# A local-attention stage whose operations are re-ordered across tiles on every engine, with the input split cut per tile and three slots for V

## The chip, the core and the metric

The kernel runs on one core of a Trainium2 chip. The core has TensorE (PE in the profile; its weight loads are PEld), VectorE (DVE), ScalarE (ACT), GpSimd (POOL), and SyncE (SP), which here only issues DMAs. Each engine works through its own list of instructions in order; semaphores tie the lists together. The metric is the device time of one execution in microseconds, the median of several. Before the change it is 907.86 us (three runs, 907.16 to 908.72). A difference under 0.2% (1.8 us) is no measurable change.

## The reference

`x` is 4 sequences of 1024 tokens with 128 features. The result is `x + s * silu(f)`, where both branches take the layer norm of `x`.

```
s: q, k, v = xn @ Wqkv.T, 16 heads of 8, rope on q and k,
   causal attention inside blocks of 32 tokens, @ Wout.T
f: two layers (DEPTH = 2), each
   h   = shift_token(x)                    # upper 64 features from the token before
   q, k, v = split(h @ wqkv)               # 8 heads of 64, INNER = 512
   q, k = l2norm(q) * qs, l2norm(k) * ksc, then rotary with xpos scaling
   sim  = 8 * q k^T, window of 64 tokens: own block and the block before, causal
   x   += softmax(sim) v @ wo              # "local attention"
   h   = layernorm(shift_token(x)) * lg + lb
   a, g = split(h @ w1 + b1)
   x   += (a * gelu(g)) @ w2 + b2
```

## The kernel before

Tokens lie along the free dimension of `X` (128 features x 4096 tokens). The program runs a small-head attention first (32 tiles of 128 tokens), and then twice a **local stage** (32 tiles of 128 tokens) and a feed-forward stage (8 chunks of 512 tokens). The change is in the local stage.

**One tile m of the local stage** goes through these operations. PE projects q, k and v (three fp32r products each, into PSUM banks 0, 1 and 2, from `split`, the input as a high and a low part). ACT squares q and k, DVE sums the squares per head, ACT makes the inverse norms of them (three tiny operations). DVE multiplies q by its cosine and sine tables and adds (`qr`), POOL scales it. DVE scales k (`kn`), POOL rotates it (`kA`, `kB`, `kr`). PE transposes `qr` and `kr` into bank 3, and ACT copies them to `qT` and `kT`. PE computes the scores into banks 4 and 5, DVE takes the maxima (`nmax`), ACT the exponentials with their sums (`prob`), DVE the reciprocals, POOL the normalised probabilities. PE transposes those in two halves (bank 6), ACT copies (`pT`), PE multiplies by the values (bank 7, called PV below), ACT copies (`oT`), PE multiplies by `wo` (bank 3 again), DVE adds the result to `X`.

**The block before.** A query block also looks at the 64 tokens before it. So each tile needs the second half of the last tile's keys in front of its own (`kT[..., 0:WIN]`), and values shifted by half a tile (`VB`). SP makes these by DMA from SBUF to SBUF. In step n of SP's list (`back`) it

1. issues the key copy of tile n, which the scores of tile n+1 wait for (semaphore `k_prev`);
2. once V of tile n is there, issues the first VB copy;
3. waits until PV of tile n-1 is done (`l_o`), since that product reads the slot of VB which is written next, and issues the second VB copy;
4. issues the two shifted copies of a finished tile of `X` into `XS[1]`, the feed-forward stage's input.

Ahead of item 1 step n waits until the `XS[1]` copies issued in step n-1 have landed. SP has one list, so all this is strictly in a row.

**Order of the work.** The lists are written out by hand: on each engine a function `local(n, par)` says what the engine does in turn n, and the turns follow each other. In the kernel before, turn n of PE is: q projection of tile n+2, q transposes of n, first probability transposes of n-1, k projection of n+2, k transposes of n, v projection of n+1, second probability transposes of n-1, scores of n, output product of n-2, PV of n-1. So PV of tile n-1 stands in the same turn as the scores of tile n. Slots alternate with the parity of the tile (V, VB, kT, qT, qr, kr, prob).

Of the kernel before, what the change touches and what calls it, by code (L numbers as in the profile page):

```python
# [78 lines left out]
def build(nc, a, out):  # L79
    with ExitStack() as ctx:  # L80
# [52 lines left out]
        V = sb("V", [P, 2, INNER])  # L133
# [101 lines left out]
        l_qk = sem("l_qk")  # L235
        l_v = sem("l_v")
        l_sq = sem("l_sq")
        l_qm = sem("l_qm")
        l_norm = sem("l_norm")
# [8 lines left out]
        l_tr = sem("l_tr")  # L248
        l_tre = sem("l_tre")
# [3 lines left out]
        l_score = sem("l_score")  # L253
        l_max = sem("l_max")
        l_exp = sem("l_exp")
        l_rinv = sem("l_rinv")
        l_prob = sem("l_prob")
        l_pT = sem("l_pT")
        l_pTe = sem("l_pTe")
# [48 lines left out]
        def _(sp):  # L308
# [49 lines left out]
            for L in range(DEPTH):  # L358
# [4 lines left out]

                def back(n, par):
                    nxt = 1 - par
                    base = L * TILES
                    turned, done = held(2 * (base + n + 1)), held(base + n + 1)
                    scored, pv1 = held(2 * (base + n)), held(base + n)
                    copied = held(xs_before_local(L) + 32 * (n - 2))
                    if live(n, -3, TILES):  # L370

                        sp.wait_ge(xs_dma, copied)
                    if live(n, 0, TILES):
                        sp.wait_ge(l_tre, turned)
                        wait(sp, l_score, scored)
                        sp.dma_start(kT[:, nxt, :, 0:WIN], kT[:, par, :, P:P + WIN]).then_inc(k_prev[nxt], 16)
                        sp.wait_ge(l_ve, done)
                        sp.dma_start(VB[64:P, par, :], V[0:64, par, :]).then_inc(v_prev[par], 16)
                        wait(sp, l_o, pv1)
                        sp.dma_start(VB[0:64, nxt, :], V[64:P, par, :]).then_inc(v_prev[nxt], 16)  # L380
                    if live(n, -2, TILES):
                        copy_shifted(XS[1], n - 2, P, x_before_local(L) + n - 1)

                if L == 0:

                    sp.wait_ge(zeros_made, 2)
                    sp.wait_ge(windows_zero, 1)
                    sp.dma_start(kT[:, 0, :, 0:WIN], kT[:, 1, :, P:P + WIN]).then_inc(k_prev[0], 16)
                    sp.dma_start(VB[0:64, 0, :], V[64:P, 1, :]).then_inc(v_prev[0], 16)
                steps(0, TILES + 1, back)  # L390
# [22 lines left out]
        def _(pe):  # L413
# [104 lines left out]
            def layer(L, tail):  # L518
# [6 lines left out]
                def project(c, hi, lo, made):  # L525

                    mm3(ps[:, c, :], hi, lo, wqkv[:, 0, c * INNER:(c + 1) * INNER],
                        wqkv[:, 1, c * INNER:(c + 1) * INNER]).then_inc(made, 1)

                def transposed(n, par, src, ready):  # L530
                    pe.wait_ge(ready, base + n + 1)
                    for c in range(4):
                        last = turn(ps[:, 3, c * P:(c + 1) * P], src[:, par, c * P:(c + 1) * P])
                    last.then_inc(l_tr, 1)

                def local(n, par):
                    nxt = 1 - par
                    now, ahead = [[split[:, (m // TPC) % 2, i, (m % TPC) * P:(m % TPC + 1) * P] for i in range(2)]
                                  for m in (n + 2, n + 1)]
                    if live(n, 2, TILES):  # L540
                        pe.wait_ge(l_split, L * CHUNKS + (n + 2) // TPC + 1)
                        wait(pe, l_qm, base + n + 2)
                        project(0, *now, l_qk)
                    if live(n, 0, TILES):

                        wait(pe, x_new, (x_before_local(L) + n - 2) if not isinstance(n, int) or n > 2 else 0)
                        transposed(n, par, qr, l_qn)

                    def scores():
                        if live(n, 0, TILES):  # L550
                            pe.wait_ge(l_tre, 2 * (base + n + 1))

                            pe.wait_ge(k_prev[par], 16 * ((base + n) // 2 + 1))
                            wait(pe, l_exp, 8 * (base + n))

                            first = 1 if par else live_mask(n)
                            half = [slice(64 * i, 64 * i + 64) for i in range(2)]
                            for w, grp in ((0, 0), (1, 1), (1, 0), (0, 1)):
                                kind = 1 if w else first
                                mm(ps[half[w], 4 + grp, :], ident_bf[half[grp], half[grp]],  # L560
                                   lmask[half[grp], bass.ds(kind * CHUNK, CHUNK)], True, False)
                            for s in range(4):
                                for w, grp in ((0, 0), (1, 1), (1, 0), (0, 1)):
                                    last = mm(ps[half[w], 4 + grp, s * P:(s + 1) * P],
                                              qT[half[grp], par, s, half[w]],
                                              kT[half[grp], par, s, 64 * w:64 * w + P], False, True)
                                    if s == 3 and w != grp:
                                        last.then_inc(l_score, 1)

                    def turned_probs(grp):  # L570
                        if live(n, -1, TILES):

                            pe.wait_ge(l_prob, 2 * (base + n - 1) + grp + 1)
                            wait(pe, l_pTe, 2 * (base + n - 1) + grp)
                            for s in range(4):
                                last = turn(ps[:, 6, s * P:(s + 1) * P], prob[:, nxt, grp, s * P:(s + 1) * P])
                            last.then_inc(l_pT, 1)

                    def output():

                        if not live(n, 0, TILES):
                            pe.wait_ge(x_new, x_before_local(L) + n - 2)
                        pe.wait_ge(l_oe, base + n - 1)
                        if live(n, 0, TILES):
                            pe.wait_ge(l_tre, 2 * (base + n + 1))
                        for c in range(4):
                            last = mm(ps[:, 3, 0:P], wo[:, c, :], oT[:, par, c * P:(c + 1) * P], c == 0, c == 3)
                        last.then_inc(l_y, 1)

                    scores_done = isinstance(n, int) and n == TILES  # L590
                    turned_probs(0)
                    if scores_done:
                        bias_products()
                        output()
                    if live(n, 2, TILES):
                        wait(pe, l_kn, base + n + 2)
# [862 lines left out]
```

## Time and profile before

| | |
|---|---|
| median of three runs | 907.86 us |
| profiled execution | 909.96 us, its span 908.2 us |
| PE busy | 800.1 us (88% of the span) |
| DVE busy | 664.4 us (73%) |
| ACT busy | 654.3 us (72%) |
| POOL busy | 523.9 us (58%) |
| mean granted TensorE clock | 0.972 |
| local stages | first maxima to last maxima: 190 to 446 us, and 551 to 808 us |

A row of a group or of the timeline names the line, the engine, the operation, output and inputs, and after an "x" how many instructions it merges. In the timeline the two numbers ahead are the start and the duration in us; the brackets at the end say how long the engine stood idle before and what released it. SPq is SP's queue, and its duration is that of the issue, not that of the transfer. `PEclk` is the granted clock: 1.00 is 2.4 GHz and 0.50 is 1.2 GHz.

### The profile page before, as it was taken

The page shows a single profiled execution, that of the slowest core. Times are in us where ns is not written, and L with a number is a line of the kernel's source. Part 1 is how long each engine was busy: PE and PEld are TensorE (multiplying, and loading weights), DVE is VectorE, ACT ScalarE, POOL GpSimd, SP SyncE. Part 2 cuts the span into 40 slices and gives each one's busy share as a digit, 9 for nine tenths or more (in the row PEclk, how much of TensorE's full clock was granted, in tenths as well). Part 3 has the DMA queues.
Part 4 walks back from the last instruction along what each step waited for, and adds up shares of the span by engine and source line. Part 5 has one row for each costly group of instructions (what it writes and reads, how often), then busy time and mean ns, then how long its engine had stood idle before and what let it go on. Part 6 is the DMA issues. An engine that isn't in the chain of part 4 may idle for free.

```text
span 908.2 us, 26049 instructions
## 1 busy us (share of the span) xinstructions
PE 800.1 (88%) x9848; PEld 610.5 (67%) x9848; DVE 664.4 (73%) x1347; ACT 654.3 (72%) x2053; POOL 523.9 (58%) x521
## 2 busy tenths in 40 slices
PE   4779999779999999999989887999999999988985
PEld 1458778557777778777756545777877777775652
DVE  1577998677887787877457767778787788745765
ACT  2337777479899899889743337989988998974463
POOL 0363333078888888888511017888888888951100
PEclk8899999889999999999999998999999999999997
DMA  9110001012222222222201121222222222222001
GB/s 308 44 45 3 4 4 41 3 47 55 57 57 63 55 58 55 60 57 63 51 18 24 29 63 37 64 53 58 57 61 56 62 52 58 58 51 100 1 36 58
DMA packets 64704, 48.24 MB, mean 53 GB/s; under 512 B 40410, under 2 KB 50948, under 8 KB 64068
## 3 DMA queue, kind: packets, MB, share of 16 engines
q1 hardware_dynamic: 64580, 46.57, 19.9%
q8 instruction: 80, 1.31, 0.6%
q14 instruction: 44, 0.36, 0.1%
HBM read 10.63 MB, written 2.10 MB: 14 GB/s over the span
## 4 chain that ended last, share of the span: by engine, by line
PE 56%; ACT 17%; DVE 16%; issue 7%; POOL 1%; DMA 1%; SPq 1%; DVEq 0%; ACTq 0%; POOLq 0%
PE ps L415 47%; PE ps L425 9%; ACT prob L880 6%; DVE nmax L1130 3%; ACT sq L822 3%; DVE nt L1158 2%; ACT V L849 2%; ACT oT L831 2%; DVE split L970 2%; ACT kT L856 1%; ACT pT L826 1%; DVE prob L1217 1%; DVE split L968 1%; DMA awo<-in_awo 1%; ACT qT L841 1%
## 5 line engine op out<-in xcount | busy, mean ns | idle before, releaser
L880 ACT ACTIVATE prob<-ps,nmax 128x128 f32<-128x128 f32 x512 | 181.8, 374 | 36.7 <-DVE nmax L1130 36.7
L415 PE MATMUL ps<-wqkv,split 128*128 128x512 f32 x576 | 188.2, 438 | 14.2 <-DVE split L970 10.1
L1348 POOL TENSOR_TENSOR prob<-prob,rinv 128x512 f32<-128x512 f32 x128 | 133.9, 1046 | 88.4 <-DVE rinv L1116 45.8
L415 PEld LDWEIGHTS ps<-wqkv,split 128*128 128x128 f32 x576 | 97.5, 195 | 33.5 <-DVE split L970 10.2
L1130 DVE TENSOR_REDUCE nmax<-ps 128x4 f32<-128x512 f32 x128 | 83.6, 686 | 48.3 <-PE ps L415 48.3
L425 PE MATMUL ps<-ident,prob 128*128 128x128 f32 x640 | 98.3, 276 | 13.9 <-POOL prob L1348 13.1
L880 ACT ACTIVATION_READ_ACCUMULATOR prob<-ps,nmax 128x1 f32 x512 | 109.0, 213 | 0.0
L1359 POOL TENSOR_TENSOR qr<-qr,ss 128x512 f32<-128x512 f32 x64 | 66.9, 1046 | 53.7 <-DVE qr L1142 53.7
L425 PEld LDWEIGHTS ps<-ident,prob 128*128 128x128 f32 x640 | 76.2, 142 | 28.3 <-POOL prob L1348 17.4
L415 PE MATMUL ps<-oT,wo 128*128 128x128 f32 x512 | 73.9, 287 | 22.0 <-ACT oT L831 22.0
L826 ACT ACTIVATE pT<-ps 128x512 f32<-128x512 f32 x128 | 80.0, 625 | 10.7 <-PE ps L425 9.1
L415 PE MATMUL ps<-split,w 128*128 128x512 f32 (+1 forms) x288 | 81.4, 427 | 6.6 <-DVE prob L1217 6.3
L415 PEld LDWEIGHTS ps<-oT,wo 128*128 128x128 f32 x512 | 62.1, 191 | 37.3 <-ACT oT L831 36.3
L822 ACT ACTIVATE sq<-ps 128x512 f32<-128x512 f32 x128 | 81.8, 640 | 5.1 <-PE ps L415 5.0
L1370 POOL TENSOR_TENSOR kr<-kA,kB 128x512 f32<-128x512 f32 x64 | 82.4, 1287 | 5.0
L1364 POOL TENSOR_TENSOR kA<-kn,lrot 128x512 f32<-128x512 f32 x64 | 81.8, 1278 | 0.0
L1313 POOL TENSOR_TENSOR qr<-ident,rstd 128x512 f32<-128x512 f32 x16 | 16.6, 1042 | 99.1 <-DVE rstd L962 96.0
L415 PEld LDWEIGHTS ps<-split,w 128*128 128x128 f32 (+1 forms) x288 | 50.4, 180 | 31.1 <-DVE prob L1217 10.1
L1330 POOL TENSOR_TENSOR prob<-D,hmask 128x512 f32<-128x512 f32 x32 | 35.1, 1097 | 59.5 <-PE ps L415 59.4
L1142 DVE TENSOR_TENSOR qr<-tA,tB 128x512 f32<-128x512 f32 x64 | 68.6, 1072 | 0.0
L415 PE MATMUL ps<-pT,VB 128*64 128x64 f32 x1024 | 66.3, 228 | 1.5 <-issue 1.5
L415 PE MATMUL ps<-kT,qT 64*64 64x128 f32 x2048 | 66.8, 269 | 0.0
(139 smaller groups left out, 1871.9 us busy)
## 6 DMA issues: line engine op xcount, KB each, us to landing
VB<-V SPq DMA_DIRECT2D x129, 128.0 KB, 2.4
kT<-kT SPq DMA_DIRECT2D x65, 128.0 KB, 2.4
XS<-X SPq DMA_DIRECT2D x32, 128.0 KB, 2.3
XS<-X SPq DMA_DIRECT2D x128, 32.0 KB, 1.9
D<-in_xT SPq DMA_DIRECT2D x8, 256.0 KB, 4.4
XS<-in_xT SPq DMA_DIRECT2D x2, 1024.0 KB, 6.7
out_T<-XS SPq DMA_DIRECT2D x8, 256.0 KB, 2.0
raw<-in_wqkv SPq DMA_DIRECT2D x2, 768.0 KB, 4.4
```

What stands on the lines that cost most here:

```text
L415: return nc.tensor.matmul(o, l, r, start=start, stop=stop, skip_group_check=True)
L425: return nc.tensor.matmul(o, i, ident[:], is_transpose=True, start=True, stop=True, skip_group_check=True)
L822: nc.scalar.activation(sq[:, c, :], ps[:, c, :], ACT.Square).then_inc(l_sq, 1)
L826: nc.scalar.activation(pT[:, grp, :], ps[:, 6, :], ACT.Copy).then_inc(l_pTe, 1)
L880: nc.scalar.activation(prob[:, par, grp, s * P:(s + 1) * P], ps[:, 4 + grp, s * P:(s + 1) * P], ACT.Exp, bias=nmax[:, par, grp * 4 + s:grp ...
L1130: v.tensor_reduce(nmax[:, par, 4 * grp:4 * grp + 4], ps[:, 4 + grp, :].rearrange("p (s k) -> p s k", s=4), AX_X, ALU.max, negate=True).the ...
L1142: v.tensor_tensor(qr[:, nxt, :], tA[:], tB[:], ALU.add).then_inc(l_qr, 1)
L1330: g.tensor_tensor(kexp[:, par, :].rearrange("p (b h k) -> p b h k", b=BLKS, h=INGRP), part(kR, n, P).rearrange("p (b k) -> p b k", b=BLKS) ...
L1348: g.tensor_tensor(p4, p4, rinv[:, slot, 4 * grp:4 * grp + 4].unsqueeze(2).broadcast_to([P, 4, P]), ALU.mult).then_inc(l_prob, 1)
L1359: g.tensor_tensor(hd(qr[:, nxt, :]), hd(qr[:, nxt, :]), ss[:, nxt, 0:8].unsqueeze(2).broadcast_to([P, HEADS, HD]), ALU.mult).then_inc(l_qn, 1)
L1364: g.tensor_tensor(hd(kA[:]), hd(kn[:]), row8(2, pos, 0, HD), ALU.mult)
L1370: g.tensor_tensor(kr[:, nxt, :], kA[:], kB[:], ALU.add).then_inc(l_kr, 1)
```

## The change

Every operation stays on its engine and is as large as before, but for one: the split of the input into high and low part, which was made for 512 tokens at a time (two operations on DVE for four tiles), is made for each tile (eight operations on DVE for four tiles), eight turns ahead. The combined semaphores are replaced by one per operation, and `V` has three slots where it had two; `VB` still has two. Each engine's turn n has a new order, and the operations in it belong to tiles that lie further apart:

| operation | tile in PE's turn n, before | after |
|---|---|---|
| q / k / v projection | n+2 / n+2 / n+1 | n+4 / n+3 / n+1 |
| q and k transposes | n | n+1 |
| scores | n | n |
| probability transposes | n-1 | n-2 |
| PV | n-1 | n-2 |
| output product | n-2 | n-4 |

There are 40 turns (-4 to 35) where there were 36 (-2 to 33). On SP the shifted copies are those of tile n-5 (before n-2). The rest of SP's list is in the same order. The core of the diff:

```
-        V = sb("V", [P, 2, INNER])
+        V = sb("V", [P, 3, INNER])
         VB = sb("VB", [P, 2, INNER])
...
                 def back(n, par):
-                    if live(n, -3, TILES):
-                        sp.wait_ge(xs_dma, copied)
+                    nxt, done = 1 - par, base + n + 1
+                    if live(n, -6, TILES):
+                        sp.wait_ge(xs_dma, xs_before_local(L) + 32 * (n - 5))
                     if live(n, 0, TILES):
-                        sp.wait_ge(l_tre, turned)
-                        wait(sp, l_score, scored)
+                        sp.wait_ge(l_tk, done)
+                        wait(sp, l_score[1], done - 1)
                         sp.dma_start(kT[:, nxt, :, 0:WIN], kT[:, par, :, P:P + WIN]).then_inc(k_prev[nxt], 16)
                         sp.wait_ge(l_ve, done)
-                        sp.dma_start(VB[64:P, par, :], V[0:64, par, :]).then_inc(v_prev[par], 16)
-                        wait(sp, l_o, pv1)
-                        sp.dma_start(VB[0:64, nxt, :], V[64:P, par, :]).then_inc(v_prev[nxt], 16)
-                    if live(n, -2, TILES):
-                        copy_shifted(XS[1], n - 2, P, x_before_local(L) + n - 1)
+                        sp.dma_start(VB[64:P, par, :], V[0:64, done % 3, :]).then_inc(v_prev[par], 16)
+                        wait(sp, l_o, done - 1)
+                        sp.dma_start(VB[0:64, nxt, :], V[64:P, done % 3, :]).then_inc(v_prev[nxt], 16)
+                    if live(n, -5, TILES):
+                        copy_shifted(XS[1], n - 5, P, x_before_local(L) + n - 4)
...
+                def scores(m):                       # PE
...
+                        pe.wait_ge(l_tq, base + m + 1)
+                        pe.wait_ge(l_tk, base + m + 1)
+                        pe.wait_ge(k_prev[m % 2], 16 * ((base + m) // 2 + 1))
...
+                def local(n, par):                   # PE
+                    q_turned(n + 1)
+                    k_projected(n + 3)
+                    probs_turned(n - 2, 0)
+                    q_projected(n + 4)
+                    k_turned(n + 1)
+                    scores(n)
+                    probs_turned(n - 2, 1)
+                    output(n - 4)
+                    v_projected(n + 1)
+                    values_summed(n - 2)
...
+                def local(n, par):                   # ACT
+                    v_copied(n)
+                    k_copied(n + 1)
+                    norm_floor(n + 3)
+                    q_squared(n + 4)
+                    norm_log(n + 3)
+                    probs_copied(n - 2, 1)
+                    norm_inverse(n + 3)
+                    exponentials(n, 0)
+                    exponentials(n, 1)
+                    q_copied(n + 2)
+                    o_copied(n - 2)
+                    k_squared(n + 4)
+                    probs_copied(n - 1, 0)
...
+                def input_high(m):                   # DVE
...
+                        v.tensor_copy(split[:, (m // TPC) % 2, 0, bass.ds((m % TPC) * P, P)],
+                                      shifted(XS[0], m, P)).then_inc(split_hi, 1)
...
+                def local(n, par):                   # DVE
+                    q_cos(n + 3)
+                    input_high(n + 8)
+                    q_sin(n + 3)
+                    inverse_sums(n - 1, 0)
+                    q_rotated(n + 3)
+                    q_summed(n + 3)
+                    k_summed(n + 3)
+                    inverse_sums(n - 1, 1)
+                    maxima(n, 0)
+                    maxima(n, 1)
+                    k_scaled(n + 3)
+                    input_low(n + 8)
+                    added_to_x(n - 4)
...
+                def local(n, par):                   # POOL
+                    q_scaled(n + 3)
+                    k_sin(n + 3)
+                    normalised(n - 1, 1)
+                    k_cos(n + 3)
+                    k_rotated(n + 3)
+                    normalised(n, 0)
```

The instructions in a row on two engines. First PE in the middle of the first local stage, before: from the scores to PV, the products `ps<-pT,VB` and `ps<-pT,V`. `ident,prob` are probability transposes, `ident,qr` and `ident,kr` those of q and k, `wqkv,split` the projections, `lmask` and `kT,qT` the scores, `oT,wo` the output product.

```order
L425 MATMUL ps<-ident,prob 128x128 [waits l_pTe,l_prob]
L425 MATMUL ps<-ident,prob 128x128 x3
L415 MATMUL ps<-lmask,ident_bf 64x512 [waits l_exp,k_prev1,l_tre]
L415 MATMUL ps<-lmask,ident_bf 64x512 x3
L415 MATMUL ps<-kT,qT 64x128 x16
L415 MATMUL ps<-oT,wo 128x128 [waits l_tre,l_oe]
L415 MATMUL ps<-oT,wo 128x128 x3
L415 MATMUL ps<-pT,VB 64x64 [waits l_ve,v_prev0,l_pTe,l_oe]
```

The same engine and place after the change:

```order
L417 MATMUL ps<-lmask,ident_bf 64x512 [waits l_exp0,k_prev1,l_exp1,l_tk,l_tq]
L417 MATMUL ps<-lmask,ident_bf 64x512 x3
L417 MATMUL ps<-kT,qT 64x128 x16
L427 MATMUL ps<-ident,prob 128x128 [waits l_pTe0,l_prob1]
L427 MATMUL ps<-ident,prob 128x128 x3
L417 MATMUL ps<-oT,wo 128x128 [waits l_tk,l_oe]
L417 MATMUL ps<-oT,wo 128x128 x3
L417 MATMUL ps<-wqkv,split 128x512 [waits l_ve,l_split]
L417 MATMUL ps<-wqkv,split 128x512 x2
L417 MATMUL ps<-pT,VB 64x64 [waits l_ve,l_pTe1,v_prev1,l_pTe0,l_oe]
```

The second probability transposes and the v projection, which stood ahead of the scores, now stand between them and PV. PV before is that of the tile one ahead of the scored one, and after that of two ahead. What PE does after PV, until the next scores, is now this:

```order
L417 MATMUL ps<-pT,V 64x64 x2
L427 MATMUL ps<-ident,qr 128x128 [waits x_new,l_qn]
L427 MATMUL ps<-ident,qr 128x128 x3
L417 MATMUL ps<-wqkv,split 128x512 [waits l_kn,l_split]
L417 MATMUL ps<-wqkv,split 128x512 x2
L427 MATMUL ps<-ident,prob 128x128 [waits l_pTe1,l_prob0]
L427 MATMUL ps<-ident,prob 128x128 x3
L417 MATMUL ps<-wqkv,split 128x512 [waits l_sqq,l_qm,l_split]
L417 MATMUL ps<-wqkv,split 128x512 x2
L427 MATMUL ps<-ident,kr 128x128 [waits l_tq,l_kr]
L427 MATMUL ps<-ident,kr 128x128 x3
L417 MATMUL ps<-lmask,ident_bf 64x512 [waits l_exp0,k_prev0,l_exp1,l_tk,l_tq]
```

Two projections and three groups of transposes are left there; before, the v projection and a fourth group stood there too.

Second, SP's list in the middle of the stage, before. `kT<-kT` is the key copy, the first `VB<-V` the copy within a tile, the second the one into the slot of the next tile, `XS1<-X` the shifted copies.

```order
L376 DMA kT<-kT 128x4x64 [waits l_score,l_tre,xs_dma]
L378 DMA VB<-V 64x512 [waits l_ve]
L380 DMA VB<-V 64x512 [waits l_o]
L348 DMA XS1<-X 64x128 [waits x_new]
L349 DMA XS1<-X 64x128
```

After the change:

```order
L378 DMA kT<-kT 128x4x64 [waits l_score1,l_tk,xs_dma]
L380 DMA VB<-V 64x512 [waits l_ve]
L382 DMA VB<-V 64x512 [waits l_o]
L353 DMA XS1<-X 64x128 [waits x_new]
L354 DMA XS1<-X 64x128
```

Nothing moved on SP, and the waits are the same kinds; but the PV and the scores between which these copies stand have moved apart on PE.

## Rows read from the trace of the kernel before

**Rows 1.** Busy us of the engines over 24 tiles of the first local stage.

```profile
223.61:422.11 198.50, 183.05 (x2424) 149.85 (x2424) 159.82 (x300) 181.17 (x649) 167.53 (x169) 1.00 0.24 58
```

**Rows 2.** Timeline of PE over one turn.

```profile
307.34 1.16 PE L415 MATMUL ps<-oT,wo 128*128 128x128 f32 x8 [0.39 <-ACT oT L831]
308.43 0.34 PE L415 MATMUL ps<-pT,VB 128*64 128x64 f32 x4
...
309.29 0.29 PE L415 MATMUL ps<-pT,V 128*64 128x64 f32 x4
309.51 0.97 PE L415 MATMUL ps<-wqkv,split 128*128 128x512 f32 x3
...
311.11 0.94 PE L415 MATMUL ps<-wqkv,split 128*128 128x512 f32 x3
311.88 0.60 PE L425 MATMUL ps<-ident,kr 128*128 128x128 f32 x4
312.26 0.96 PE L415 MATMUL ps<-wqkv,split 128*128 128x512 f32 x3
313.06 0.60 PE L425 MATMUL ps<-ident,prob 128*128 128x128 f32 x4
313.59 0.41 PE L415 MATMUL ps<-lmask,ident_bf 64*64 64x512 bf16 x4
...
315.27 1.16 PE L415 MATMUL ps<-oT,wo 128*128 128x128 f32 x8 [0.39 <-ACT oT L831]
```

**Rows 3.** Timeline of SP's queue after a PV, and at tile 30.

```profile
309.62 0.46 SPq L380 DMA_DIRECT2D VB<-V  x1
310.12 0.60 SPq L348 DMA_DIRECT2D XS<-X  x1
310.76 0.60 SPq L349 DMA_DIRECT2D XS<-X  x1
...
433.80 0.60 SPq L349 DMA_DIRECT2D XS<-X  x1
435.79 0.63 SPq L376 DMA_DIRECT2D kT<-kT  x1
```

**Rows 4.** The page's DMA issues: count, KB, median us from issue to landing.

```profile
kT<-kT SPq DMA_DIRECT2D x65, 128.0 KB, 2.4
```

**Rows 5.** Timeline of DVE: maxima of tiles 0 and 31, both layers.

```profile
190.12 1.29 DVE L1130 TENSOR_REDUCE nmax<-ps 128x4 f32<-128x512 f32 x2 [0.19 <-PE ps L415]
...
446.43 1.29 DVE L1130 TENSOR_REDUCE nmax<-ps 128x4 f32<-128x512 f32 x2 [4.08 <-PE ps L415]
...
550.75 1.29 DVE L1130 TENSOR_REDUCE nmax<-ps 128x4 f32<-128x512 f32 x2 [0.84 <-PE ps L415]
...
807.90 1.29 DVE L1130 TENSOR_REDUCE nmax<-ps 128x4 f32<-128x512 f32 x2 [4.08 <-PE ps L415]
```

**Rows 6.** Windows of 6 us from the start of a PE gap: busy, PEclk, DMA.

```profile
64.90:70.90 6.00, 2.52 (x43) 0.78 0.00 0
...
552.00:558.00 6.00, 3.64 (x39) 1.00 0.02 5
...
893.70:899.70 6.00, 3.19 (x6) 0.84 0.12 44
36.50:42.50 6.00, 4.54 (x16) 1.00 0.19 44
```

**Rows 7.** Timeline of PE behind the gap that ends at 193.74.

```profile
193.74 0.66 PE L425 MATMUL ps<-ident,prob 128*128 128x128 f32 x4 [2.35 <-POOL prob L1348]
194.15 1.26 PE L415 MATMUL ps<-wqkv,split 128*128 128x512 f32 x3
195.21 1.05 PE L425 MATMUL ps<-ident,kr 128*128 128x128 f32 x4
195.92 1.63 PE L415 MATMUL ps<-wqkv,split 128*128 128x512 f32 x3
197.34 0.92 PE L425 MATMUL ps<-ident,prob 128*128 128x128 f32 x4
```

More of the change, by code:

```diff
@@ L536, in local @@
[L536 to L557, printed above, removed]
-                            for w, grp in ((0, 0), (1, 1), (1, 0), (0, 1)):
[L559 to L585, printed above, removed]
@@ new lines, in scores @@
+                def scores(m):
+                    if 0 <= m < TILES:
+                        if m == 0:
+                            if L == 0:
+                                pe.wait_ge(a_done, TILES)
+                            else:
+                                pe.wait_ge(ffn_hid, NPART * L * CHUNKS)
+                        pe.wait_ge(l_tq, base + m + 1)
+                        pe.wait_ge(l_tk, base + m + 1)
+                        pe.wait_ge(k_prev[m % 2], 16 * ((base + m) // 2 + 1))
+                        wait(pe, l_exp[0], 4 * (base + m))
+                        wait(pe, l_exp[1], 4 * (base + m))
+                        first, par = min(m % TPB, 1), m % 2
+                        half = [slice(64 * i, 64 * i + 64) for i in range(2)]
+                        for w, grp in ((0, 0), (1, 1), (1, 0), (0, 1)):
+                            kind = 1 if w else first
+                            mm(ps[half[w], 4 + grp, :], ident_bf[half[grp], half[grp]],
+                               lmask[half[grp], bass.ds(kind * CHUNK, CHUNK)], True, False)
+                        for s in range(4):
+                            for w, grp in ((0, 0), (1, 1), (1, 0), (0, 1)):
+                                last = mm(ps[half[w], 4 + grp, s * P:(s + 1) * P],
+                                          qT[half[grp], par, s, half[w]],
+                                          kT[half[grp], par, s, 64 * w:64 * w + P], False, True)
+                                if s == 3 and w != grp:
+                                    last.then_inc(l_score[grp], 1)
@@ new lines, in probs_turned, with output @@
+                def probs_turned(m, grp):
+                    if 0 <= m < TILES:
+                        pe.wait_ge(l_prob[grp], base + m + 1)
+                        wait(pe, l_pTe[1 - grp], base + m + grp)
+                        for s in range(4):
+                            last = turn(ps[:, 6, s * P:(s + 1) * P], prob[:, m % 2, grp, s * P:(s + 1) * P])
+                        last.then_inc(l_pT[grp], 1)
+                def output(m):
+                    if 0 <= m < TILES:
+                        if m == 0:
+                            pe.wait_ge(wo_in, 16 * (L + 1))
+                        pe.wait_ge(l_oe, base + m + 1)
+                        if 0 <= m + 5 < TILES:
+                            pe.wait_ge(l_tk, base + m + 5 + 1)
+                        elif 0 <= m + 5 < TILES:
+                            pe.wait_ge(l_tq, base + m + 5 + 1)
+                        elif 0 <= m - 1 < TILES:
+                            pe.wait_ge(x_new, x_before_local(L) + m - 1 + 1)
@@ L586, in output @@
                         for c in range(4):
[L587 removed]
+                            last = mm(ps[:, 3, 0:P], wo[:, c, :], oT[:, m % 2, c * P:(c + 1) * P], c == 0, c == 3)
                         last.then_inc(l_y, 1)
[L590 to L594, printed above, removed]
@@ L864, in local, with o_copied, norm_floor @@
+                def o_copied(m):
+                    if 0 <= m < TILES:
+                        act.wait_ge(l_o, base + m + 1)
+                        wait(act, l_y, base + m - 1)
+                        nc.scalar.activation(oT[:, m % 2, :], ps[:, 7, :], ACT.Copy).then_inc(l_oe, 1)
+                def norm_floor(m):
+                    if 0 <= m < TILES:
+                        act.wait_ge(l_nq, base + m + 1)
+                        act.wait_ge(l_nk, base + m + 1)
                         nc.scalar.activation(lognt[:, 0, :], nt[:], ACT.Relu, bias=floor[:, 0:1]).then_inc(l_floor, 1)
-                    if live(n, -2, TILES) and not scores_done:
-                        output()
```

466 lines of the change are left out of this document (248 added, 218 removed).

## The prediction

> **What bounds the kernel now.** I read the share of busy time first, then the local stage by windows, then PE's timeline over one turn, then SP's queue, because what the change moves apart on PE is tied together by copies on that queue.
>
> The local stages make up 513 of the 908 us: from the first maxima to the last 256.3 us in the first layer and 257.2 us in the second [rows 5], for 31 intervals each. In the regular middle 24 tiles take 198.5 us, 8.27 us a tile. In them PE is busy 183.1 us, ACT 181.2, POOL 167.5 and DVE 159.8 [rows 1], so per tile 7.63, 7.55, 6.98 and 6.66 us. PE is the bound, nearly: one turn is 315.27 - 307.34 = 7.93 us, with one idle stretch of 0.39 us ahead of the output product, until ACT has copied `oT` [rows 2]. Without it a turn would be 7.54 us.
>
> SP's queue is not late before. After a PV it issues the second VB copy and the two shifted copies and then waits anyway, for the next tile's `kT` [rows 3]; the scores that wait for that key copy come almost a turn after it.
>
> **What the change does to that queue.** The loop to look at runs: PV of tile n-1, then on SP the second VB copy, the two shifted copies of tile n-5, the wait until these have landed, the key copy of tile n+1, then on PE the scores of tile n+2. Before, PV of tile n-1 was in turn n and those scores in turn n+2; what closed the loop was PV of tile n+1 in the same turn, so one pass advanced by two tiles and had two turns of time. After, PV of tile n-1 is in turn n+1, and behind the scores of tile n+2 comes PV of tile n, in the same turn n+2. One pass now advances by one tile only. A third V slot does nothing for it: VB has two slots still, and the queue is as strict as it was.
>
> The length of one pass, step by step:
> - PV ends at 309.29 + 0.29 = 309.58 [rows 2], the VB copy is issued at 309.62 [rows 3]: 0.04.
> - VB copy to first shifted copy 0.50, to the second 0.64 [rows 3].
> - Second shifted copy, issued at 433.80, to the key copy at 435.79 [rows 3]: 1.99. This is the one place of the regular kind where `kT` was ready first, so that the landing is what the queue waited for.
> - Key copy, issue to landing: 2.4 [rows 4].
> - PE: scores 315.27 - 313.59 - 0.39 = 1.29; four probability transposes 313.59 - 313.06 = 0.53; output product 308.43 - 307.34 = 1.09; v projection 313.06 - 312.26 = 0.80; PV until its end 309.58 - 308.43 = 1.15 [rows 2]. Together 4.86.
>
> SP's part is 5.57, the pass 10.43 us. That is above the 8.27 us of now and above what any engine needs. What PE has to do between PV and the next scores (two projections, three groups of transposes) took 312.26 - 309.51 = 2.75 us before [rows 2], so it ends long before the key copy lands, and PE then stands idle for about 5.57 - 2.75 + 0.07 = 2.9 us in every turn.
>
> The first shifted copy is issued in SP's step 5 and waited for first in step 6. Up to the scores of tile 6 a pass has neither the 0.64 nor the 1.99: 10.43 - 2.63 = 7.8 us. So of 31 intervals 6 cost 7.8 (46.8 us in all) and 25 the full pass.
>
> **The clock.** I then looked at what such a gap of PE does to its granted clock. The trace has nine gaps of PE of 2 us or longer (after the start of the kernel), at 64.9, 168.6, 176.4, 191.4, 516.4, 544.2, 552.0, 559.7 and 893.7. Over the six microseconds from their start the mean clock was 0.78 for the first and 0.84 for the last, and it stayed 1.00 only at 552.0; behind the five gaps of about 1.5 us, the first at 36.5, it was 1.00 [rows 6]. In eight of nine cases, then, the clock went down to its 1.2 GHz level and came back later. Behind the gap that ends at 193.74 the slow stretch reaches from about 194.2 to the transposes at 197.34, which still show 0.92 instead of 0.60 [rows 2, 7]: some 3.5 us of work. There k projection to k transposes took 195.21 - 194.15 = 1.06 where it takes 0.77, and those transposes 0.71 where they take 0.38 [rows 2, 7]. Work runs at about half speed, so 3.5 us of it lose 1.75. In the changed kernel the fall comes with the end of the gap, which is the start of the scores, and the slow stretch lies on the part of PE's turn that is in the loop. I take off 0.25 for falls that begin inside the gap and count eight in nine: 1.5 x 8/9 = 1.33 us a tile. The pass becomes 11.76 us.
>
> [...]
>
> **The other edits.**
> - Removed wait: the 0.39 us ahead of the output product goes, since its `oT` is now of four tiles back. Next late is the key copy, so this is worth nothing.
> - Order on ACT, DVE and POOL: with 7.55, 6.66 and 6.98 us of work in a turn of 11.8 each has over 4 us of room, and what the scores, transposes and PV take from them is made a turn ahead or in PE's gap. No cost. In a turn of 7.54 ACT would have no room at all; that matters only in the last rival.
> - Split per tile: eight instructions for four tiles instead of two. DVE's price per tile is unknown, between nothing and 1 us; either way hidden by DVE's 5 us of free time. Cost 0; without the cover up to 1 us x 64.
> - Third V slot and single semaphores: they take a wait from ACT that is not late. 0.
> - SP: the same five issues per step. The waits for V and `kT` are met before SP comes to them.
> - Filling and draining: four more turns per layer. At the start PE transposes the keys of tile 1 before it scores tile 0, so POOL's work on one more tile (6.98 us) lies ahead; I take 6. At the end there are two more passes through bank 3 (an output product, 1.16 us, and an addition each), and PV of the last tile waits for one more pass of SP's queue; I take 4. Together 10 a layer, between 0 (the attention's and the feed-forward's last work cover it) and 17; a gain is excluded, since turns are only added.
>
> **The sum.** A layer: 46.8 + 25 x 11.76 = 340.8 us from first to last maxima. Against 256.3 and 257.2 that is +84.5 and +83.6, together +168. With 20 for the ends it is +188 on the profiled execution's 909.96: 1098 us. The median of the runs is 2.1 us below the profiled execution, so 1096 us. Its own range: at a loss of 1.0 to 2.0 us a tile from the clock, and 0 to 34 for the ends, about 1060 to 1135.
>
> **Rivals.**
> - *The clock holds.* The gap of 2.9 us is there, but the matmuls around it keep the clock up, as at 552.0. The pass is 10.43: 46.8 + 260.8 = 307.6 a layer, +51.3 and +50.4, with the ends +122: 1030 us. For it: one case in nine, and a clock of 1.00 through the whole of rows 1. Against: the other eight.
> - *The landing of the shifted copies is not in the pass.* If SP could go on to the key copy at once, the pass would be 8.44 and the gap about 0.9 us, too short for the clock: 46.8 + 211.0 = 257.8, +2 over both layers, with the ends 930 us. For it: only one place shows the 1.99, and there the pieces of SP may have met by chance. Against: the wait is written ahead of the key copy, and it needs the copies just issued.
> - *The queue never decides, and PE runs without a gap (faster).* The place is the same: the key copy. If it is there when PE comes to the scores, a turn is 7.54 us: 31 x 7.54 = 233.7, -22.6 and -23.4, with the ends 26 us faster: 882 us. It decides from a pass under 7.54 on, which needs SP's part to be 2.7 us, half of what I read. For it: PE has 7.54 us of work, and all the other loops that I followed (bank 3, the norms, the probabilities) have time in such a turn. Against: the four rows of SP's part, each measured.
>
> **Chances.** The forecast 0.62, the clock holds 0.20, landing not in the pass 0.10, faster 0.08. A measurement of this kernel tells 0.2% (1.8 us) from no change. Faster then comes to 0.07, within it 0.01, slower 0.92. The range reaches down to the clock's rival and up to the top of the forecast's own: 1015 to 1135.
>
> **What would show it.** In the changed profile: turns of 7.8 us up to tile 6, then 11 to 12.5 us; PE busy far below 88% of a longer span; one idle stretch of 2.5 to 3 us per turn ahead of `lmask`, released by a DMA; a mean clock near 0.85 and 0.5 in many half-microseconds behind those gaps; SP's key copy 2 us behind the second shifted copy in every step, where before that happened rarely. The wait for `oT` is gone. It would be wrong if PE waited ahead of the scores for an engine, or if the key copy were issued early in the turn, and mis-sized if turns were near 10.4 with the clock at 1.00.

## The result and the profile after

The changed kernel takes 1070.11 us (median of four runs, 1065.85 to 1079.05) against 907.51 us: 1.180 times as long, 95% interval 1.1725 to 1.188. 1096 us were predicted, in a range of 1015 to 1135. The profiled execution has a span of 1066.9 us where it had 908.2.

The page: its busy times, and the granted clock in 40 slices.

```profile
span 1066.9 us, 26797 instructions
PE 830.5 (78%) x9848; PEld 633.6 (59%) x9848; DVE 677.9 (64%) x1443; ACT 646.6 (61%) x2053; POOL 549.4 (51%) x521
...
PEclk7999998799899989997799989999999999889997
```

The work is what it was: PE is busy 30 us more, most of it work at a low clock (a turn at a low clock below has 10.2 us of PE busy, a regular one 7.45); the other engines' busy times are near the old ones. The span has grown by 159 us, so nearly all of it is waiting. This is PE's timeline over one turn, in the stage's regular part; it answers to [rows 2].

```profile
331.16 0.60 PE L427 MATMUL ps<-ident,kr 128*128 128x128 f32 x4
334.49 0.41 PE L417 MATMUL ps<-lmask,ident_bf 64*64 64x512 bf16 x4 [2.73 <-issue]
...
335.70 0.66 PE L427 MATMUL ps<-ident,prob 128*128 128x128 f32 x4
336.19 1.06 PE L417 MATMUL ps<-oT,wo 128*128 128x128 f32 x8
337.01 0.95 PE L417 MATMUL ps<-wqkv,split 128*128 128x512 f32 x3
337.88 0.34 PE L417 MATMUL ps<-pT,VB 128*64 128x64 f32 x4
...
338.75 0.29 PE L417 MATMUL ps<-pT,V 128*64 128x64 f32 x4
338.96 0.66 PE L427 MATMUL ps<-ident,qr 128*128 128x128 f32 x4
...
344.65 0.41 PE L417 MATMUL ps<-lmask,ident_bf 64*64 64x512 bf16 x4 [2.72 <-issue]
```

The turn is 344.65 - 334.49 = 10.16 us. 2.7 of them PE stands ahead of the scores (`lmask`). On PE's rows the profile puts the wait down to "issue", that is, to nothing it shows. ACT waits for the same key copy before it writes the next `kT`, and there the page does name it:

```profile
L874 ACT ACTIVATE kT<-ps 128x512 f32<-128x512 f32 x64 | 39.0, 609 | 122.1 <-DMA kT<-kT 113.3
```

SP's queue over the same stretch, which answers to [rows 3], says what it is:

```profile
339.07 0.46 SPq L382 DMA_DIRECT2D VB<-V  x1
339.58 0.60 SPq L353 DMA_DIRECT2D XS<-X  x1
340.22 0.60 SPq L354 DMA_DIRECT2D XS<-X  x1
342.13 0.63 SPq L378 DMA_DIRECT2D kT<-kT  x1
```

PV ends at 338.75 + 0.29 = 339.04, the second VB copy goes out 0.03 later, the shifted copies after 0.51 and 0.64, the key copy 1.91 behind the second of them, and the scores start 2.52 behind that. Together 5.61, and PE from the scores to the end of PV 4.55: 10.16 us, the turn.

The starts of the scores give all turns, here from tile 0 to tile 31, in us (a list made from the timeline; the bar stands behind tile 6):

```
before,  layer 0: 188.78 to 445.08 = 256.30
after,   layer 0: 202.41 to 518.18 = 315.77
   6.77 6.97 7.49 7.72 7.95 7.69 | 10.16 12.02 12.94 11.74 10.16 10.15 10.14 10.18 10.16
   10.14 10.12 10.19 10.17 10.14 12.98 11.74 10.17 10.12 10.31 10.19 10.17 10.15 12.80
   11.61 12.53
before,  layer 1: 549.27 to 806.55 = 257.28
after,   layer 1: 644.27 to 956.22 = 311.95
   6.25 6.95 7.52 7.52 8.15 7.67 | 10.25 11.72 10.17 10.15 10.13 10.42 10.21 10.15 10.14
   10.18 10.17 10.14 10.58 11.88 11.80 10.14 10.18 10.20 10.30 11.26 11.76 11.70 10.17
   12.61 11.48
```

The six first turns of a layer are short, and behind them a turn takes about 10.15 us or more. 16 of the 50 are over 11 us, and they are of two kinds. 14 of them are at a low clock (0.76 to 0.87 over the turn) and lose 2 us each, 27 us together. The other two, 11.88 and 11.26 us in the second layer, have a clock of 1.00 and PE's usual busy time, so the pass itself was longer: the shifted copies landed late, and the key copy was issued 3.62 and 3.00 us behind the second of them. The gap of PE behind such a turn is 4.44 and 3.85 us, and the turn after it is at a low clock. Windows of the changed kernel (per engine the busy time, then PEclk, DMA share and GB/s): a stretch after a gap, a stretch of about one turn, 100 us in the middle, the turn of 11.88 us and the one behind it.

```profile
257.00:262.00 5.00, 4.84 (x51) 4.19 (x51) 2.78 (x6) 3.77 (x16) 1.72 (x3) 0.66 0.06 14
271.58:284.50 12.92, 10.18 (x102) 8.42 (x103) 7.37 (x14) 7.52 (x27) 7.34 (x7) 0.76 0.15 36
300.00:400.00 100.00, 73.19 (x965) 60.57 (x964) 63.48 (x135) 70.92 (x256) 71.39 (x68) 0.97 0.20 47
822.74:834.62 11.88, 7.45 (x101) 6.15 (x102) 6.63 (x14) 7.39 (x28) 7.43 (x7) 1.00 0.17 41
834.62:846.42 11.80, 9.00 (x103) 7.59 (x103) 6.62 (x14) 7.53 (x28) 7.42 (x7) 0.86 0.16 39
```

SP's queue in the turn of 11.88 us, and PE behind it:

```profile
828.46 0.60 SPq L354 DMA_DIRECT2D XS<-X  x1
832.08 0.63 SPq L378 DMA_DIRECT2D kT<-kT  x1
834.62 0.41 PE L417 MATMUL ps<-lmask,ident_bf 64*64 64x512 bf16 x4 [4.44 <-issue]
```

Nor are the gaps all alike. In the last turns of a layer PE has no more projections to make for later tiles, and its gaps grow to 3.4 to 3.65 us. Behind the 40 gaps of 2.4 to 3.1 us 7 turns are at a low clock; behind the 8 of 3.4 to 4.4 us 7 are, and the eighth is at 0.92.

The 159 us come from: the stages +59.5 and +54.7; the way to the first scores +13.6, of which 2.5 to 3.3 us arose in the small-head attention, which the change leaves alone (its last output product starts at 176.52 us here and at 173.3 to 174.1 in the kernels of the first three experiments); from the last scores of the first layer to the first of the second +21.9 (126.1 against 104.2); the end +9.0.

### The profile page after: what moved, and what is told of

The parts are those of the page before. It is cut to its first block, busy times and chain, and to the rows that moved or that the text cites. A ratio compares the mean times of both kernels' runs of the same rounds, so it can differ in the third digit from the quotient of the medians.

```text
span 1066.9 us, 26797 instructions
## 1 busy us (share of the span) xinstructions
PE 830.5 (78%) x9848; PEld 633.6 (59%) x9848; DVE 677.9 (64%) x1443; ACT 646.6 (61%) x2053; POOL 549.4 (51%) x521
## 4 chain that ended last, share of the span: by engine, by line
PE 65%; issue 20%; DVE 11%; ACT 3%; DMA 1%; SPq 1%; POOL 0%; DVEq 0%; ACTq 0%
PE ps L417 52%; PE ps L427 13%; DVE split L1177 1%; DVE nt L1204 1%; DVE prob L1295 1%; DVE nt L1210 1%; DMA awo<-in_awo 1%; DVE vexp L1095 1%; ACT pT L889 1%; ACT prob L921 1%; DVE kn L1216 0%; DVE tA L1184 0%; DVE tB L1191 0%; DVE lrot L1117 0%; DVE tB L1190 0%
## 5 line engine op out<-in xcount | busy, mean ns | idle before, releaser
L417 PE MATMUL ps<-lmask,ident_bf 64*64 64x512 bf16 x256 | 29.2, 441 | 146.8 <-issue 146.6
L921 ACT ACTIVATION_READ_ACCUMULATOR prob<-ps,nmax 128x1 f32 x512 | 115.5, 226 | 0.0
L874 ACT ACTIVATE kT<-ps 128x512 f32<-128x512 f32 x64 | 39.0, 609 | 122.1 <-DMA kT<-kT 113.3
L427 PE MATMUL ps<-ident,prob 128*128 128x128 f32 x640 | 106.9, 293 | 3.1 <-ACT pT L889 3.1
L1443 POOL TENSOR_TENSOR kA<-kn,lrot 128x512 f32<-128x512 f32 x64 | 104.2, 1628 | 0.0
L417 PEld LDWEIGHTS ps<-lmask,ident_bf 64*64 64x64 bf16 x256 | 9.0, 107 | 159.9 <-issue 159.9
L1457 POOL TENSOR_TENSOR kr<-kA,kB 128x512 f32<-128x512 f32 x64 | 85.0, 1328 | 5.0
L417 PE MATMUL ps<-kT,qT 64*64 64x128 f32 x2048 | 79.9, 300 | 0.0
L417 PEld LDWEIGHTS ps<-kT,qT 64*64 64x64 f32 x2048 | 72.9, 152 | 4.8 <-issue 2.1
L417 PEld LDWEIGHTS ps<-oT,wo 128*128 128x128 f32 x512 | 71.0, 214 | 1.4 <-issue 1.3
```

Source lines behind the costliest of these rows:

```text
L417: return nc.tensor.matmul(o, l, r, start=start, stop=stop, skip_group_check=True)
L427: return nc.tensor.matmul(o, i, ident[:], is_transpose=True, start=True, stop=True, skip_group_check=True)
L874: nc.scalar.activation(kT[:, m % 2, :, WIN:WIN + P], ps[:, 3, :].rearrange("p (c t) -> p c t", c=4), ACT.Copy).then_inc(l_tk, 1)
L921: nc.scalar.activation(prob[:, m % 2, grp, s * P:(s + 1) * P], ps[:, 4 + grp, s * P:(s + 1) * P], ACT.Exp, bias=nmax[:, m % 2, col], accum ...
L1443: g.tensor_tensor(hd(kA[:]), hd(kn[:]), row8(2, m, 0, HD), ALU.mult).then_inc(l_km, 1)
L1457: g.tensor_tensor(kr[:, m % 2, :], kA[:], kB[:], ALU.add).then_inc(l_kr, 1)
```

## The experiments

**The second VB copy one step later.** If the pass through SP's queue sets the turn, it must go once PV and the next key copy are no longer in one step. Two things move: the copy with its wait for PV, and the wait for the landing.

```
 def back(n, par):
-    if live(n, -6, TILES): sp.wait_ge(xs_dma, ...)          # landed
     if live(n, 0, TILES):
         ... key copy of tile n
+    if live(n, -1, TILES):
+        sp.wait_ge(l_ve, done - 1)
+        wait(sp, l_o, done - 2)
+        sp.dma_start(VB[0:64, par, :], V[64:P, (done - 1) % 3, :])
     if live(n, 0, TILES):
         ... first VB copy of tile n
-        wait(sp, l_o, done - 1)
-        sp.dma_start(VB[0:64, nxt, :], V[64:P, done % 3, :])
+    if live(n, -6, TILES): sp.wait_ge(xs_dma, ...)          # landed
     if live(n, -5, TILES): copy_shifted(...)
```

> The changed kernel, with SP's second VB copy of tile n-1 moved into step n, behind the key copy of tile n, and the wait for the landing of the shifted copies moved to just ahead of the next shifted copies. Nothing else differs. Theory (the queue pass sets the turn): one pass from PV over the key copy to the next PV then advances by two tiles, about 9.5 us for two turns, and PE's own 7.54 us become the bound. Turns of 7.6 us in place of 10.15 (and 11.7 to 12.9 with a low clock), TensorE idle ahead of the scores near 0, clock near 1.00 in the stage. 31 x 7.6 = 235.6 us a layer, 42 us less than before over both, and some 35 us more for filling and draining as the changed kernel shows them: about 900 us. Rival 1 (the gap ahead of the scores has another source, ACT's wait for the key copy or the norms): turns stay near 10, 1060 us. Rival 2 (ACT, with 7.55 us of busy time in a tile, is the next bound): turns of 8 us or more, 925 us or more.

Measured: 889.75 us, 0.980 of the kernel before (0.9786 to 0.9816), and so 180 us faster than the changed kernel. I expected about 900. The stages are 227.1 and 228.7 us from first to last scores where I had 235.6. The turns are 7.46 us, 7.3 where the split has run out, and 6.5 to 6.8 at the end. Its windows over 171.4 us of the first layer, and its timelines of PE and SP:

```profile
223.60:395.00 171.40, 170.49 (x2305) 139.30 (x2305) 152.76 (x317) 167.82 (x620) 169.43 (x161) 1.00 0.27 63
```

```profile
331.79 0.41 PE L420 MATMUL ps<-lmask,ident_bf 64*64 64x512 bf16 x4
...
339.24 0.41 PE L420 MATMUL ps<-lmask,ident_bf 64*64 64x512 bf16 x4
```

```profile
336.41 0.46 SPq L380 DMA_DIRECT2D VB<-V  x1
336.93 0.59 SPq L383 DMA_DIRECT2D VB<-V  x1
337.61 0.55 SPq L353 DMA_DIRECT2D XS<-X  x1
338.22 0.60 SPq L354 DMA_DIRECT2D XS<-X  x1
338.91 0.63 SPq L376 DMA_DIRECT2D kT<-kT  x1
```

PE is busy 170.5 of 171.4 us, at full clock, and there is no idle stretch ahead of the scores. The key copy at 338.91 comes 0.3 us ahead of scores that do not need it: they start at 339.24, and what they read was copied a turn earlier. Both rivals fall: neither ACT nor the norms hold PE. So the new order itself is good for turns of 7.46 us in place of 8.27, below the 7.54 I had for PE; what cost 180 us is where two waits of SP's list stand. The next experiment moves one of the two alone; the second VB copy alone was not moved.

**Only the landing wait moved.**

```
 def back(n, par):
-    if live(n, -6, TILES): sp.wait_ge(xs_dma, ...)          # ahead of the key copy
     ... key copy, first VB copy, wait for PV, second VB copy
+    if live(n, -6, TILES): sp.wait_ge(xs_dma, ...)          # ahead of the shifted copies
     if live(n, -5, TILES): copy_shifted(...)
```

> The changed kernel, with only the wait for the landing of the shifted copies moved: from ahead of SP's key copy to just ahead of the next shifted copies. The second VB copy still waits for PV. Theory: the pass loses the 1.91 us between the second shifted copy and the key copy (340.22 to 342.13 in the changed kernel's trace) and keeps the rest, so turns of 10.15 - 1.91 = 8.24 us from tile 7 on, a PE gap of 0.8 us, and no fall of the clock in the stage. 44.6 + 25 x 8.24 = 250.6 us a layer where the changed kernel has 316 and 312: about 940 us. Rival (the copies issued just now do not hold the key copy; something else in the queue does): 1060 to 1070 us.

Measured: 989.70 us, 1.089 of before (1.087 to 1.091). The rival falls, and the sizes were off: 50 us above what I expected. Regular turns are 8.95 us where I had 8.24. SP's queue and PE in this kernel:

```profile
358.72 0.46 SPq L380 DMA_DIRECT2D VB<-V  x1
359.28 0.54 SPq L353 DMA_DIRECT2D XS<-X  x1
359.86 0.60 SPq L354 DMA_DIRECT2D XS<-X  x1
360.56 0.63 SPq L376 DMA_DIRECT2D kT<-kT  x1
```

```profile
363.10 0.41 PE L417 MATMUL ps<-lmask,ident_bf 64*64 64x512 bf16 x4 [1.52 <-issue]
```

From the second shifted copy to the key copy it is 0.70 us in place of 1.91: the wait is gone, the time of the issue itself stays, which I had left out. 10.15 - 1.21 = 8.94, the turn. That is the pass confirmed by its size, and 0.71 us in each of 50 turns is 35 us of what I missed. Ten of the fifty turns are longer, 9.97 to 10.88 us. Eight of them are at a low clock (0.82 to 0.86) and cost 12 us; in the other two (9.97 and 10.49 us, clock 1.00) the scores start 3.35 and 4.06 us behind the key copy in place of 2.5. The regular gap of 1.5 us is not what the low clock stands behind. Seven of the eight follow gaps of 2.25 to 2.54 us, most of them in the last turns of a layer, and one follows a gap of 1.96 us. A gap of 3.04 us had no such turn behind it. A regular turn and one of the last turns of the layer:

```profile
372.03:380.98 8.95, 7.46 (x103) 6.17 (x103) 6.63 (x14) 7.41 (x28) 7.44 (x8) 1.00 0.23 55
454.62:465.18 10.56, 7.79 (x95) 6.41 (x96) 1.93 (x5) 5.99 (x23) 3.51 (x4) 0.82 0.19 44
```

**PE's gap filled.** Eight products more in each of 50 gaps.

```
                         wait(pe, l_exp[0], 4 * (base + m))
                         wait(pe, l_exp[1], 4 * (base + m))
+                        if m >= 7:
+                            for _ in range(8):
+                                mm(ps[:, 4, :], ident_bf[:], lmask[:, 0:CHUNK])
+                        pe.wait_ge(k_prev[m % 2], 16 * ((base + m) // 2 + 1))
```

> The changed kernel, with eight added products (128x512, bf16, into bank 4, overwritten by the scores) in PE's gap ahead of the wait for the key copy, for tiles 7 to 31 of each layer. They are about 1.7 us of extra work in a gap of 2.7 us. Theory of the clock: the turns of 11.5 to 12.9 us are those of 10.15 us at the low clock, and with PE busy in the gap they go: 25 x 10.15 a layer, 298 us in place of 316 and 312, about 1035 us in all, 3% faster though work was added. Rival (the long turns come from the queue or from DMA and not from the clock): 1070 us or slower.

Measured: 1038.87 us, 1.1452 of before (1.1398 to 1.1507), 31 us less than the changed kernel although each layer has 200 products more. PE in a turn of it:

```profile
397.90 1.67 PE L417 MATMUL ps<-lmask,ident_bf 128*128 128x512 bf16 x7
400.40 0.41 PE L417 MATMUL ps<-lmask,ident_bf 64*64 64x512 bf16 x4 [0.83 <-DMA kT<-kT]
```

Four of the fifty turns are still over 11 us (11.30, 13.15, 12.01, 11.03). Only that of 13.15 us is at a low clock, 0.87; in all four the key copy went out 2.8 to 3.9 us behind the second shifted copy in place of 1.9, so what is left there is late landing. The mean clock of the four executions is 0.962 to 0.968, and 0.926 to 0.937 in the changed kernel. So filling the gap took away 13 of the 14 turns at a low clock, which cost the changed kernel 27 us.

The 31 us are not that term alone. The stages are 302.7 and 298.1 us from first to last scores, 26.9 us less together. In them regular turns are 10.0 us, 0.15 less than before (the scores now start 2.37 us behind the key copy, not 2.52), which is 7 us for 50 turns, and the turn of 13.15 and the late landings take about as much back. The rest of the difference lies outside the turns that the edit touches. Here, too, the profile names the releaser of the scores, where it said "issue" before: the key copy.

**Only the split per tile, in the kernel before.**

```
                     maxima(0)
-                    if live(n, 3, TILES) and (n + 3) % TPC == 0:
-                        split_into(j % 2, shifted(XS[0], j, CHUNK), CHUNK, l_split, L * CHUNKS + j)
+                    input_high(n + 6)
                     maxima(1)
+                    input_low(n + 6)
```

> The kernel before, with one part of the change alone: the input split per tile, six tiles ahead, the high part between the two maxima and the low part behind them. Theory: before, every fourth turn is 9.30 us in place of 7.93, since the split of 512 tokens (0.68 and 1.65 us on DVE) stands between the two maxima; per tile the pieces are 0.2 and 0.3 us and the turns become 7.93 to 8.0. Seven or eight long turns a layer lose 1.37 us each: 15 x 1.37 = 21 us less, about 888 us. Rival (the pieces delay the second maxima in every turn by 0.2 us and with it the exponentials, which are on the chain): 8.1 to 8.2 us a turn, 900 to 905 us.

Measured: 905.61 us, 0.9971 of before (0.9961 to 0.998): faster by 0.3%, and the rival, 900 to 905 us, was near. The turns are 8.26 us each, where they were 7.93, 7.93, 7.93 and 9.30 with a mean of 8.27. DVE's timeline says why:

```profile
346.58 0.69 DVE L1146 TENSOR_REDUCE nmax<-ps 128x4 f32<-128x512 f32 x1 [0.56 <-PE ps L415]
347.19 0.59 DVE L1119 CAST split<-XS 128x128 fp32r<-128x128 f32 x1
347.69 0.68 DVE L1146 TENSOR_REDUCE nmax<-ps 128x4 f32<-128x512 f32 x1
```

From first to second maxima it is 347.69 - 346.58 = 1.11 us, and 0.60 where nothing stands between them. The high part of 128 tokens takes 0.5 us there, though it is a quarter of the work that took 0.68. I had priced it at 0.2 us, and that is what it takes (0.22) at the start of the stage, where POOL is idle; in the regular turns POOL is at work on `kB` and `kr` meanwhile, and it takes 0.57 to 0.60. Why is not shown. The cast of 512 tokens, too, took 0.41 or 0.42 us in the kernel before beside an idle POOL and 0.68 beside a working one. Cut into tiles and left on the chain, the split costs nearly the same as before. What gains is to take it off the chain.

**The end of the stage.** To the kernel with the VB copy later (889.75 us):

```
PE    local(TILES + 1, 1); variance(2, 2, 0); norm_bcast(0, ...); local(TILES + 2, 0)
      norm_bcast(1, ...); local(TILES + 3, 1)
DVE   links(2, 1, 6, 2); scaled(0, tA); local(TILES + 2, 0); links(2, 7, 9, 2)
      local(TILES + 3, 1); links(2, 10, NEWTON, 2)
```

> The kernel with the second VB copy a step later (889.75 us), with the feed-forward stage's first steps woven back into the last turns: on PE the third variance and the first broadcast stand ahead of turn 34 and the second broadcast ahead of turn 35, on DVE the links of the third chunk and the first scaled chunk between the last additions to X. Theory (part of what the ends cost is this order: from the last addition to the first up projection the changed kernel takes 5.4 us, 541.05 to 546.46, the kernel before 2.6 us, 459.42 to 461.98): 2.8 us less per layer, 884 us. Rival (the last additions are late for their own chain, PV of the last tile, and the woven steps only delay them): 889 to 891 us.

Measured: 888.13 us (885.6 to 892.42), not to be told from 889.75. I expected 884. From the last addition to the first up projection it is now 2.56 us (449.58 to 452.14), but the last addition has moved from 19.6 to 21.6 us behind the start of the last scores. The rival was right. What is late there is the last tile itself. This kernel's timeline:

```profile
433.75 1.04 POOL L1431 TENSOR_TENSOR prob<-prob,rinv 128x512 f32<-128x512 f32 x1 [0.36 <-DVE rinv L1233]
...
439.86 0.63 PE L430 MATMUL ps<-ident,prob 128*128 128x128 f32 x4
```

Tile 31's probabilities are ready at 434.79 and PE transposes the first of them at 439.86, because its list has the whole of turn 32 first: tiles that lie further apart drain later.

**The start of the stage.** In the kernel of the last experiment DVE now sums q's and k's squares ahead of `q_rotated` in the turns below 0.

> The same kernel as the one before it in this call, and in turns -3 to -1 of each layer DVE sums the squares of q and k before it adds the rotated q, not after. Theory (filling runs from kn to kn: k projection, its square, the sums, the norm's three steps, kn, 7.0 us a turn, and DVE's addition of qr, up to 1.67 us beside POOL, stands in the middle of it): about 1.3 us less in each of three turns of two layers, 7.8 us, some 876 us if the call's other kernel is at 884. Rival (the loop is not what sets the fill; POOL's 5.9 us of work on a tile is): less than 2 us of difference between the two.

Measured: 884.83 us (884.27 to 889.32), 0.976 of before (0.9738 to 0.9781): 3.3 us less than the kernel without this order, by medians whose ranges overlap; I expected 7.8. The first interval from `kn` to `kn`, in the first layer 7.02 us (180.09 to 187.11), is 5.61; the next is 7.06 (185.18 to 192.24) as before, and in the second layer even 7.82 for 6.93. ACT's timeline in that one:

```profile
187.67 0.60 ACT L864 ACTIVATE sq<-ps 128x512 f32<-128x512 f32 x1 [2.11 <-PE ps L420]
190.41 0.60 ACT L877 ACTIVATE kT<-ps 128x512 f32<-128x512 f32 x1 [2.15 <-PE ps L430]
190.91 0.30 ACT L904 ACTIVATE lognt<-nt,floor 128x16 f32<-128x16 f32 x1
```

DVE's sums end at 188.32 + 0.67 = 188.99, but on ACT the norm's first step stands behind the copy of `kT`, and so waits for PE's transposes until 190.91. The next wait took the place of the one removed; whether another order there would shorten it was not tried.

## Why the prediction was right, point by point

- **The bound before**: PE, nearly. With the waits gone the new order reaches 7.46 us a turn; I had worked out 7.54.
- **The pass through SP's queue**: right in mechanism, place and size. Each term has its row: 0.04 was 0.03, 0.50 was 0.51, 0.64 was 0.64, 1.99 was 1.91, 2.4 was 2.52 with the start of the scores. PE's part, 4.86, was 4.55, mostly the output product and v projection with 1.69 for 1.89. 10.43 was 10.15, and over 50 turns that is 14 us. The second experiment took 1.21 us from the pass and the turn fell by 1.2; the first took the pass away and the turn fell to PE's own work.
- **The 1.99 us for the landing**: a near number read from the wrong row. I took the key copy at 435.79 [rows 3] for one that waited for the landing because `kT` was ready first. It was not:

```profile
435.07 0.66 ACT L856 ACTIVATE kT<-ps 128x512 f32<-128x512 f32 x1
```

  ACT ended that `kT` at 435.73, and the key copy went out 0.06 us later, as in every regular step before the change. So the row shows `kT` and not the landing, and that it came within 0.08 us of the 1.91 measured is luck. That a landing takes about that long stands elsewhere, in the page's 1.9 us for the 32 KB copies `XS<-X`.
- **The first six turns**: 88.7 us over both layers for 93.6, but not for my reason. With the pass mended (first experiment) the same six turns take 43.9 and 45.7 us, and in the changed kernel PE has no gap ahead of their scores but one of 0.15 us. The pass did not set them; that its 7.8 us came near is luck.
- **The gap of PE**: 2.7 us for 2.9.
- **The clock**: this is the term that was mis-sized. I took a loss of 1.33 us in each of 50 turns, 67 us, from "eight in nine". What the turns hold above 10.15 us is 315.77 - 44.59 - 253.75 = 17.4 in the first layer and 14.1 in the second, 32 us; 27 of them are the clock, 3 the two late landings, and the rest is small. The mechanism is there, but in 14 turns of 50, which lose 2 us each, and often in runs of two or three behind one another; in between, stretches of ten and eleven turns with much the same gap kept 1.00. The mean clock came out at 0.933 and not near 0.85. The eight cases of [rows 6] were gaps in stretches that are irregular around them; the regular turn is another case, and I had no row for it. Three of the nine gaps, too, were shorter than the 2 us that I named: in PE's timeline they are 1.86 us (at 168.6), 1.59 (at 544.2) and 1.98 (at 559.7), and the mean clock behind them was 0.72, 0.72 and 0.79. So 2 us is no bound. What decides which turns are hit is open; all that the runs show is that the gaps above 3.4 us had nearly all such a turn behind them and the shorter ones seldom, and most of the long gaps lie in turns in which PE also has less work.
- **Filling and draining**: too small by half. 20 us were predicted, 13.6 + 21.9 + 9.0 = 44.5 measured, beyond my bound of 34. In the profiled executions of the first three experiments, whose first and last turns are as in the changed kernel, it is 37 to 38, beyond the bound too. I counted one POOL tile ahead of the first scores. But PE's turn 0 has the k projection of tile 3 and the q projection of tile 4 ahead of the scores of tile 0, and each turn of the filling runs from `kn` to `kn` in 7.0 us. At the end I counted passes through bank 3 and missed that the last tile's probabilities wait a whole turn of PE. These causes are read from the lists and the timelines; the last two experiments touched them and moved 0 to 3 us. The two misses, 35 us too many for the clock and 24.5 too few for the ends, partly cancel.
- **The other edits at nothing**: right for ACT, DVE and POOL, with one exception seen only in the last experiments: in the filling their orders count.
- **The range**: its upper end by my own terms (a loss of 2.0 us in 50 turns, 34 us for the ends) is 1143 us and not 1135; the measurement lies well inside either.
- **The rivals**: "the clock holds" was 1030 us, and the third experiment comes near its world with 1038.87. "The landing is not in the pass" was priced 930, and the kernel that makes it so takes 990: 25 us of that because a turn is 8.95 us and not 8.44 (the issue stays), the rest mostly low clock in eight turns and dearer ends. "The queue never decides" was priced 882, and the kernel with the queue mended takes 889.75.

The sum by measured terms: 88.7 + 50 x 10.15 + 31.6 - 513.6 = 114.2, and 44.5 for the ends: 158.7 us, the difference of the spans.

## What to carry to other kernels

When a schedule spreads one tile's operations over more turns, take each queue that is strictly in order, DMA queues first, and ask by how many tiles one pass through it advances; the turn is at least the pass divided by that number, whatever the busy times say. Here two tiles became one and a pass of 10.15 us went from free to being the bound, and moving one copy and one wait within SP's list turned 18% slower into 2% faster. Then price the ends on their own: four turns more in each of two layers cost 37 to 45 us here, about a quarter of the loss. And before a row is taken for a wait, look what else ended just ahead of it.

## What the runs showed of the hardware

In the changed kernel PE's clock was low in 7 turns behind 40 gaps of 2.4 to 3.1 us, and in 7 behind 8 gaps of 3.4 to 4.4 us, with the eighth at 0.92. With regular gaps of 1.5 us it was low in 8 turns of 50, seven of them behind gaps of 2.25 to 2.54 us and one behind 1.96. PE kept busy with discarded products for 1.7 us of the 2.7 had one such turn left in 50, and the kernel was 31 us faster.

A copy whose landing usually takes 1.9 us now and then takes 1 to 2 us longer: twice in 50 turns of the changed kernel (3.62 and 3.00 us to the next issue), four times in 50 with the filled gap (2.81 to 3.90). Why is not shown.

A DVE cast of 128x128 from fp32 took 0.22 us beside an idle POOL and, in the regular turns with POOL at work, 0.57 to 0.66; a cast of 128x512 took 0.41 or 0.42 us and 0.68.

A wait for a DMA can stand in the profile as "issue": PE's 2.7 us ahead of the scores had no releaser in the changed kernel, and had the key copy as releaser in the kernel with the filled gap.
